# A transformer layer on one core: loads of the projection's last chunk issued behind later query stores

## The reference, cut to what matters

```python
qkv = hidden_states @ Wqkv
scores = einsum('bqhd,bkd->bhqk', q, k) * scale
scores = where(causal, scores + alibi, NEG_INF)
attn = einsum('bhqk,bkd->bqhd', softmax(scores), v).reshape(B, S, H)
x = layernorm(x + attn @ Wo)
x = layernorm(x + x @ fake_int4(weight).T + bias)
```

## Time and profile before

| | us |
|---|---|
| median of 3 runs | 2289.73 |
| the runs | 2285.76, 2289.73, 2289.76 |
| span of the profiled execution, first to last instruction | 2283.8 |
| its own device time, with what lies around the span | not given; the runs are 2.0 to 6.0 above the span |
| mean granted clock of TensorE in the span | 0.992 |
| PE busy / DVE / ACT / POOL | 2235.8 / 1662.1 / 999.3 / 919.2 |

### The profile page before, as it was taken

One profiled execution on the slowest core, in us unless ns is written; L12 is line 12 of the kernel. 1 busy time (PEld: TensorE's weight loads), 2 busy tenths in 40 slices (PEclk: granted clock), 3 DMA queues, 4 the chain that ended last, 5 costly groups with the idle time before them and its releaser, 6 DMA issues.

```text
span 2283.8 us, 36024 instructions
## 1 busy us (share of the span) xinstructions
PE 2235.8 (98%) x12280; PEld 1519.5 (67%) x12280; DVE 1662.1 (73%) x5002; ACT 999.3 (44%) x1950; POOL 919.2 (40%) x558
## 2 busy tenths in 40 slices
PE   7999999899999999999999999999999999999998
PEld 6888888655555555555555555547888888888886
DVE  6977768868888888888888888836555555555554
ACT  4222222157777777777777777760101010101010
POOL 0000000047888788887888787861010101101010
PEclk9999999989999999999999999999999999999999
DMA  6555553644433442443233323256232333232320
GB/s 223 194 180 188 196 192 134 183 109 104 108 79 96 113 103 77 105 108 99 59 94 90 81 68 95 58 203 162 75 101 83 101 83 98 86 98 85 93 73 28
DMA packets 179837, 257.02 MB, mean 113 GB/s; under 512 B 15446, under 2 KB 105686, under 8 KB 179306
## 3 DMA queue, kind: packets, MB, share of 16 engines
q1 hardware_dynamic: 179510, 254.87, 38.3%
q10 hardware_dynamic: 180, 0.33, 0.0%
HBM read 166.89 MB, written 87.20 MB: 111 GB/s over the span
## 4 chain that ended last, share of the span: by engine, by line
PE 71%; ACT 4%; DVE 3%; issue 1%; SPq 1%; DMA 0%; POOL 0%; ACTq 0%; POOLq 0%; DVEq 0%
PE pf L1392 30%; PE pa L1130 12%; PE pa L240 12%; PE pa L1114 11%; PE pa L1154 5%; ACT probs L1219 4%; DVE xm L259 2%; PE pf L1417 1%; DMA xk<-recip_d 0%; SPq L1292 0%; PE pa L249 0%; POOL probs L1085 0%; POOL probs L1071 0%; DVE probs L1240 0%; DVE late L1259 0%
## 5 line engine op out<-in xcount | busy, mean ns | idle before, releaser
L1219 ACT ACTIVATE probs<-pa,slope 128x512 f32<-128x512 f32 (+3 forms) x1536 | 773.5, 588 | 245.2 <-PE pa L1114 154.5
L259 DVE CUSTOM_DVE_ANT_0 xm<-pa,xm 128x128 bf16<-128x128 f32 (+1 forms) x1488 | 750.7, 554 | 137.5 <-PE pa L240 124.0
L1085 POOL TENSOR_TENSOR probs<-probs 128x1024 f32<-128x1024 f32 x252 | 686.7, 2725 | 108.7 <-PE pa L1130 87.3
L1489 POOL TENSOR_TENSOR yb<-y,xm 128x1024 f32<-128x1024 f32 x32 | 76.6, 2395 | 659.8 <-DVE z L1502 644.5
L1130 PE MATMUL pa<-probs,v 128*32 128x512 f32 (+3 forms) x3072 | 308.6, 497 | 2.9 <-POOL probs L1071 2.9
L1446 ACT ACTIVATE ln<-ln 128x1 f32<-128x1 f32 x64 | 13.0, 203 | 498.8 <-DVE ln L1522 498.8
L1071 POOL TENSOR_SCALAR_AFFINE_SELECT probs<-probs 128x512 f32<-128x512 f32 x256 | 159.4, 635 | 108.0 <-ACT probs L1219 108.0
L1392 PE MATMUL pf<-ff_lo,xk 128*128 128x512 f32 x512 | 200.4, 391 | 0.0
L1064 POOL MEMSET credit<- 128x1 f32 x4 | 0.2, 98 | 468.7 <-POOLq L348 468.7
L656 ACT ACTIVATE q_hi<-ps,qscale 128x512 fp32r<-128x512 f32 x64 | 43.9, 688 | 292.1 <-PE ps L552 276.9
L1392 PE MATMUL pf<-fo_hi,xk 128*128 128x512 f32 x512 | 166.8, 397 | 0.0
(11 more groups left out here) (154 smaller groups left out, 4283.5 us busy)
## 6 DMA issues: line engine op xcount, KB each, us to landing
xm<-in_L_attn_hidden_states SPq DMA_DIRECT2D x8, 2048.0 KB, 9.3
q_hi_d<-q_hi SPq DMA_DIRECT2D x64, 256.0 KB, 2.0
q_lo_d<-q_lo SPq DMA_DIRECT2D x64, 256.0 KB, 2.5
att_d<-att SPq DMA_DIRECT2D x64, 256.0 KB
xm<-in_L_attn_hidden_states SPq DMA_DIRECT2D x32, 512.0 KB, 3.7
out<-z SPq DMA_DIRECT2D x32, 512.0 KB, 2.6
q<-q_hi_d SPq DMA_DIRECT2D x62, 256.0 KB, 6.0
xq<-q_hi_d SPq DMA_DIRECT2D x44, 256.0 KB, 5.7
```

The lines of the kernel that those rows point to most:

```text
L259: nc.vector.tensor_tensor_reduce(out=unused[:, 0:keys], in0=bank[:, 0:keys], in1=sh.distance[:, d0:d0 + keys], scale=1.0, scalar=-3e38, op ...
L1085: nc.gpsimd.tensor_tensor(o, o, probs[:, source % PR, h0:h1, 0:N], ALU.add).then_inc(add_done, 1)
L1219: nc.scalar.activation(probs[:, n % PR, h, 0:N], sc_ps[sc_ring.bank[use]][:, at:at + N], ACT.Exp, scale=slope[:, bass.ds(g * HPG + h, 1)]) ...
L1489: nc.gpsimd.tensor_tensor(yb[:, :], y[:, u, :], bias[:, :], ALU.add).then_inc(yb_done, 1)
```

## The change

The second half of iteration 0's queries is no longer in `load_first`; it has a semaphore of its own, `second_in`, and is issued behind the store of index 2. The five row loads are issued behind the store of index 3, and what is left of `load_second` behind the store of index 4 (before, rows and `load_second` stood behind the store of index 1). PE waits for `second_in` just before the first piece that reads the second half (piece 16, use 16). A memset on POOL adds to `loaded[0]` what the three moved loads used to add, so that all waits on it keep their numbers; it has one more column in `credit`.

```diff
-LOADS, FIRST_HALF = 16 * (3 * HALF + 2), 16 * (3 + 1)
+LOADS, FIRST_HALF, SECOND_HALF = 16 * (3 * HALF + 2), 16 * (3 + 1), 16 * 3
...
-        self.distance_in, self.slope_in = sem("distance_in"), sem("slope_in")
+        self.distance_in, self.slope_in, self.second_in = sem("distance_in"), sem("slope_in"), sem("second_in")
...
-        seven, credit = sb("seven", [P, KT]), sb("credit", [P, 6])
+        seven, credit = sb("seven", [P, KT]), sb("credit", [P, 7])
...
                 sp.dma_start(raw(sh.k3[0][0:3 * D, :]), k_d[:, 0:S]).then_inc(sh.loaded[0], 16)
-                load_queries(sp, first_q, q_hi_d, q_lo_d, 0, sh.loaded[0])
+                load_queries(sp, first_q, q_hi_d, q_lo_d, 0, sh.loaded[0], (0,))
                 sp.dma_start(sh.distance, distance_h).then_inc(sh.distance_in, 16)
 
-            def load_second():
+            def load_second_half():
+
+                load_queries(sp, first_q, q_hi_d, q_lo_d, 0, sh.second_in, (1,))
+
+            def load_first_rows():
 
                 load_rows(sp, sh, first_q, sh.k3[0], rows_d, 0)
                 load_rows(sp, sh, (sh.q1,), sh.k3[1], rows_d, 1, (0,))
+
+            def load_second():
+
                 sp.dma_start(raw(sh.k3[1][0:3 * D, :]), k_d[:, 0:S]).then_inc(sh.loaded[1], 16)
                 load_queries(sp, (sh.q1,), q_hi_d, q_lo_d, 1, sh.loaded[1], (0,))
                 sp.dma_start(sh.slope[:, :], slope_h).then_inc(sh.slope_in, 16)
...
-                    if last and c == 1:
+                    if last and c == 2:
+                        load_second_half()
+                    if last and c == 3:
+                        load_first_rows()
+                    if last and c == 4:
                         load_second()
...
+            pool.memset(credit[:, 6:7], 0.0).then_inc(sh.loaded[0], SECOND_HALF)
...
             def first_maximum(use):
 
+                if FIRST[use] == ("piece", BPH * HPG):
+                    pe.wait_ge(sh.second_in, SECOND_HALF)
                 if use >= 2:
                     pe.wait_ge(sh.mx_free, use - 1)
```

## The result

| | us |
|---|---|
| kernel before, median of 21 runs | 2288.61 (2284.79 to 2290.32) |
| changed kernel, median of 21 runs on the same chips | 2285.55 (2281.08 to 2287.98) |
| ratio | 0.9985, 95% interval 0.9979 to 0.9992 |
| the profiled execution of the changed kernel: span / own time | 2283.8 / 2285.55 |

The change takes 3.1 us, 0.13% of the time; by the interval it is between 1.8 and 4.8 us. The forecast was 2.8 us. Some executions ran in a slow state that no edit explains: three of the kernel before in later batches and one of e10, at 2364 to 6393 us, are left out of every figure here.

The account below looks back on a forecast made before the run. PE was taken to bound the kernel, with a hole before use 2 caused by a late query store. DVE's 1.6 us plus 1.2 us of clock gave 2.8 us, from 2289.73 to 2286.9 us, range 2285.8 to 2288.1.

Parts of the forecast that it names:

- What bounds: Last projection chunk: PE idles 3.85 us before use 2, through loads, late first query store, ACT q_hi, DVE q_lo.
- The first half's queue: Ahead of the first query store: three loads leave, the store lands 2.1 to 3.5 us earlier, DVE gains 1.60 us.
- ACT's wait shrinks to 5 us or less: Sign that the forecast is right: ACT's wait for the first query store falls from 8.44 us.
- The clock: Behind use 2: PE's slow stretch at 1.2 GHz costs 2.33 us; half, 1.2 us, taken to come back.
- The added wait: PE's new wait for second_in at use 16: cost 0, with 5 us of cover.
- The third rival: Second half not there at use 16: PE stands 2.4 us plus up to 2.3 of clock, 2291.6 us; chance 0.05.
- The rest at nothing: SP's issues, later loads, put_max, the POOL memset and the rest of the kernel: no cost, later work shifts along.
- Sum: Whole kernel: 1.6 + 1.2 = 2.8 us gained, ends 1.6 and 3.9, giving 2286.9 us from a median of 2289.73.
- the second rival: Only DVE's 1.6 us or less, as the clock still falls or the store gains less; 2288.1 to 2289.7 us; chance 0.25.
- Its own range: Whole kernel: the forecast's range of 2285.8 to 2288.1 us, for a gain of 1.6 to 3.9; chance 0.42.
- the range over all cases: Whole kernel: forecast range widened to the rivals, 2282.6 to 2289.8 us.
- the first rival: Shift meets a luckier clock, nearly all of 2.33 us back: 2281.9, or 2283.0 us with 2.8; chance 0.28.

Follow-up runs that it names:

- e10: Kernel before, no load moved, with the pieces of the first maxima three groups of matmuls later and put_max cut in two; 2284.4 us, ratio 0.9977 to 0.9996.
- e2: Changed kernel with the second half's loads put back ahead of the first query store, only rows and the rest of load_second later; 2286.9 us, ratio 0.9989 to 1.0007.
- e1: Changed kernel with only the second half's loads moved; rows, keys, queries and slope back behind the store of index 1; 2291.3 us, ratio 1.0004 to 1.0022.
- e4: Changed kernel with the last int4 step done for 1 of 8 groups (result wrong, for timing only); 2282.1 us, ratio 0.9959 to 0.9985.
- e11: Changed kernel with seven of eight groups of the last int4 step omitted and the wo stores behind the first query store; 2283.1 us, ratio 0.9971 to 0.9988.
- e3: Changed kernel with the two wo stores (1 MB) also issued behind the first query store; 2284.4 us, ratio 0.9972 to 0.9990.
- e13: The changed kernel itself run again, source of its second profile; 2285.1 us, ratio 0.9976 to 0.9993 to the kernel before.
- e9: Changed kernel with put_max cut in two and the pieces left in place; 2284.5 us, ratio 0.9976 to 0.9994 to the kernel before.
- e7: Changed kernel with every piece of the first maxima three groups of matmuls later and put_max cut in two; 2280.8 us, ratio 0.9954 to 0.9980.
- e5: Kernel before with 11 extra unread matmuls of 512 columns in front of use 2, no load moved; 2286.0 us, ratio 0.9980 to 0.9998.
- e6: Changed kernel with 7 extra unread matmuls of 512 columns in front of use 2; 2283.1 us, ratio 0.9968 to 0.9989 to the kernel before.
- e12: Changed kernel with pieces four groups later, put_max cut in two, last chunk's v transposes behind product 2; 2279.9 us, ratio 0.9954 to 0.9980.

## Why the prediction was right

- **What bounds.** The chain of loads, first query store, ACT's q_hi, DVE's q_lo and PE's use 2 was right. e2 leaves the front of the queue as it was and heals nothing; e1 clears it and the store is early; e4 makes the store the late one again, and e11 takes away both.
- **The first half's queue.** Foretold: the store lands 2.1 to 3.5 us earlier, 1.60 us of it usable, q_lo right behind the int4 work. Measured: 2.5 us earlier (6.7 against 9.2), no pause of q_lo, hole 2.14 us (2.25 foretold), 1.71 us gained up to use 2 in the second profile. e3 confirms that a further 2.6 us is wasted, as the step said of the rest. The Trainium skill's page "DMA: Bandwidth & Descriptors", in its table of the cost components of one DMA (a fit for DMAs issued from GpSimd), gives an estimate of 1.8 us for these bytes, below what the trace shows; the measured 2.5 us for 786,432 bytes is 315 GB/s, between the rates of my stretches.
- **Where this step misread a row.** It said that no stretch moved more than 380 GB/s. The stretch 416 to 418 of the kernel before moved 413 (shown above). At that rate the loads are worth 1.9 us, the store lands at 418.7 and q_hi ends at 419.4, still before DVE is free at 419.78, so the 1.60 us stand. The sign "ACT's wait shrinks to 5 us or less" came from the upper end alone; the wait was 5.93 us, which is 8.44 less the 2.5.
- **The clock.** Foretold: 2.33 us of cost, half of it back. Measured: full-clock work takes 6.48 us (6.54 foretold); in e13 7.78 us, 1.09 back of 2.33; in the first profile all. My bounds were right. The half was a choice between them without a source, and that it came near is luck in part. One of my two reasons for it, that a hole of 2.25 us keeps the clock in some runs, was not seen: in all three profiles with a hole of 2.14 to 2.16 us at this place (e13, e3, e9) the clock fell. The other, that the fall can hardly last as long, is what happened: it was half as long (1.7 us lost in each of the three, against 3.4). It did not fall where the hole was 0.55 us: PE's pause before the transposes of v, 1.8 to 2.5 us, sometimes drops the clock by itself, makes PE late for use 2 and so fills the hole. In such a run the two terms trade: 1.08 and 2.39 us instead of 1.71 and 1.09.
- **The added wait.** Foretold at nothing with 5 us of cover: the second half landed 5.1 us after issue, 5.1 us ahead of use 16. The third rival named this place, the wait and the clock behind it; e1 is that rival, called forth by undoing two of the three moves: 4.45 us idle, a fall of the clock, slower than before. The rival's price of 4.7 us was for a wait of 2.4. With 4.45 in its place the same sum gives 6.8 us; the tail of e1 is 6.9 us longer than that of the first profile of the changed kernel, which is its twin up to use 2 (0.55 and 0.52 us idle).
- **The rest at nothing.** The cut of put_max changes nothing (e9), and in both profiles of the changed kernel PE stands no more than 0.36 us at any place between use 16 and the end of the block, as in the kernel before.
- **Sum.** 2.8 us foretold, 3.1 measured, tails 2.7 and 3.4. The interval of 1.8 to 4.8 us tells the forecast from DVE's 1.60 us alone (the second rival), but not from 1.60 with the whole 2.33 of the clock; that split rests on the profiles. The absolute forecast of 2286.9 is 1.35 above the result, mostly because the median of the first three runs of the kernel before, 2289.73, was 1.1 above that of 21. Its own range of 2285.8 to 2288.1 missed the result by 0.25; the range over all cases held it. That range ended at 2282.6, though the first rival's own figure was 2281.9, so it was drawn 0.7 too narrow. The first rival's luckier clock is what one profile shows, but the medians of 21 and 11 runs, 2285.6 and 2285.1, lie above its 2283.0. And 0.2% was too coarse for what can be told: 21 runs of each kernel give 0.07% to either side.

## What to carry to other kernels

A load queued ahead of a store is a dependency that the program does not show: find what the late store waits behind, and move away only what is needed later. A load moved back needs its own queue cleared as well, or the wait returns at its new place (e1). When two engines are each late at one point, as the store and the int4 work are here, removing one yields at most the distance to the other; then it can be cheaper to ask for the result later, as e7 does, than to hasten it.

## What the runs showed of the hardware

- Work that nothing reads made the kernel before 2.0 us faster (e5, interval 0.02 to 0.20%). In its profile PE's clock stayed at 2.4 GHz behind use 2, where it fell to 1.2 GHz in the kernel before, after a hole of 3.85 us.
- The length of a pause alone does not decide whether the clock falls. Before the transposes, pauses of 1.82 to 2.33 us kept it at 1.00 in nine of the profiles (the longest in e2), and pauses of 2.42 to 2.51 us were followed by half clock in all three that had them (the changed kernel's first, e1, e6); but 2.00 us in e5 was followed by 0.50 as well (404 to 406). Before use 2, 2.14 to 2.16 us (e13, e3, e9) were followed by half clock, and 2.29 us in e10 were not. The Trainium skill's page "TensorE: Matmul & The Clock Gate" says in its part on the warm-up that the moment of a change is not tied to the kernel's start; these runs agree.
- DMAs ahead of a store in the same queue delayed it: 786,432 bytes of loads were worth 2.5 us (315 GB/s) and 1 MB of stores 2.6 us (e3, 400 GB/s), while taking away what was queued behind it gained nothing (e2).
- At the end of the attention the slow stretch differed between executions, with no edit near it: the clock of 1520 to 1525 was 0.57 in the first profile of the changed kernel, while that of 1510 to 1525 was 1.00 in e12 and e11. What the clock lacks to 1.00 in 1505 to 1525 adds up to one of four values in the 14 profiles: nothing, 1.7, 3.4 or 5.1 us, whatever the kernel. This one place can so add or take as much as the change is worth.
